# Cross-attention Mamba block and expert layer: placing arithmetic, bias and skip terms, silu batches, TensorE order and scatters rearranged

## Time and profile before

| | DVE | PE | POOL | ACT |
|---|---|---|---|---|
| busy, us of the span of 312.6 | 218.2 | 264.2 | 218.7 | 170.0 |
| busy from 19.68 to 162.0, us of 142.3 | 125.3 | 106.8 | 113.6 | 88.0 |

### The profile page before, as it was taken

The page is one execution under the profiler, slowest core; times in us unless marked ns, Lnnn a source line. Parts: engine busy times, 40 slices in busy tenths (PEclk is TensorE's granted clock), DMA queues, the critical chain, the costliest instruction groups (busy, mean ns, idle before and its releaser), DMA issues. The chain is left out here.

```text
span 312.6 us, 4937 instructions
## 1 busy us (share of the span) xinstructions
PE 264.2 (85%) x1520; PEld 232.9 (75%) x1520; DVE 218.2 (70%) x383; ACT 170.0 (54%) x367; POOL 218.7 (70%) x182
## 2 busy tenths in 40 slices
PE   8969877886957947697699899999999999999960
PEld 7748665755746636576488799999999999999950
DVE  2489999987699788998945346857575757566610
ACT  1678579463893457638404347646473737373410
POOL 1839699959939699698371686677777777777652
PEclk9995989596796976756559999999999999999995
DMA  6459540052001442110055144454555454644011
GB/s 171 172 142 338 167 170 0 3 191 113 0 17 54 163 155 122 51 53 0 34 199 181 64 103 163 176 210 167 209 167 208 166 207 165 208 166 167 33 40 38
DMA packets 14929, 40.24 MB, mean 129 GB/s; under 512 B 2906, under 2 KB 9756, under 8 KB 11968
## 3 DMA queue, kind: packets, MB, share of 16 engines
q1 hardware_dynamic: 11648, 33.02, 31.2%
q0 software_dynamic: 2816, 6.32, 5.8%
q10 hardware_dynamic: 448, 0.70, 0.9%
HBM read 32.58 MB, written 8.49 MB: 131 GB/s over the span
## 5 line engine op out<-in xcount | busy, mean ns | idle before, releaser
L342 POOL TENSOR_TENSOR dbu<-du,bsb 128x1024 f32<-128x1024 f32 x31 | 72.5, 2359 | 6.2 <-ACT bsb L515 3.6
L1131 DVE TENSOR_TENSOR_SCAN h<-ps,dbu 128x512 f32<-128x512 f32 x64 | 74.5, 1206 | 1.1 <-ACT ps L529 0.7
L529 ACT ACTIVATE ps<-delta,anegs 128x255 f32<-128x255 f32 x128 | 53.0, 462 | 7.5 <-DVE h L1131 7.3
L1296 DVE SCALAR_TENSOR_TENSOR htlo<-ps,hthi 128x320 fp32r<-128x320 f32 x64 | 30.5, 487 | 35.2 <-ACT hthi L655 35.2
L766 PE MATMUL ps<-cst,hc 128*128 128x128 f32 x256 | 48.4, 351 | 0.0
L749 PE MATMUL ps<-stack,sels 64*128 64x256 f32 x64 | 19.5, 393 | 33.1 <-DVE hc L1142 29.6
L426 POOL TENSOR_TENSOR w2lo<-w2raw,w2hi 128x512 fp32r<-128x512 f32 x30 | 38.4, 1303 | 9.8 <-ACT w2hi L646 9.6
L766 PEld LDWEIGHTS ps<-cst,hc 128*128 128x128 f32 x256 | 39.4, 182 | 4.6 <-issue 2.2
L749 PEld LDWEIGHTS ps<-stack,sels 64*128 64x128 f32 x64 | 12.3, 239 | 40.6 <-issue 40.5
L935 PE MATMUL ps<-hthi,w2hi 128*128 128x320 f32 x128 | 40.3, 315 | 0.0
L935 PE MATMUL ps<-xthi,w1hi 128*128 (+1 forms) x128 | 40.2, 314 | 0.0
(11 more groups left out here) (149 smaller groups left out, 482.1 us busy)
## 6 DMA issues: line engine op xcount, KB each, us to landing
w1raw<-in_w SPq DMA_DIRECT2D x8, 1024.0 KB
w2raw<-in_w SPq DMA_DIRECT2D x8, 1024.0 KB, 4.8
bsb<-b_rows SPq DMA_DIRECT2D x7, 1024.0 KB, 7.3
expert_rows<-fill SPq DMA_DIRECT2D x1, 2580.0 KB, 15.9
xe<-expert_rows SPq DMA_DIRECT2D x8, 258.0 KB, 5.3
out<-x SPq DMA_DIRECT2D x4, 256.0 KB, 4.9
xnat<-in_x SPq DMA_DIRECT2D x1, 768.0 KB, 7.4
xe<-expert_rows SPq DMA_DIRECT2D x8, 64.5 KB, 5.5
```

The lines of the kernel that those rows point to most:

```text
L342: nc.gpsimd.tensor_tensor(dbu[j % DRING][:], du[:, :, None, cols(b)].to_broadcast([P, EC, 2, L]), bsb[b % 2][:, None, 2 * p:2 * p + 2, :]. ...
L529: ins = nc.scalar.activation(decays(g % SLOTS_DA)[:, c, i * L + 1:(i + 1) * L], delta[:, c, b * L + 1:(b + 1) * L], ACT.Exp, scale=anegs[: ...
L1131: nc.vector.tensor_tensor_scan(h[g % HRING][:, c].rearrange("p n t -> p (n t)"), decays(g % SLOTS_DA)[:, c, :], dbu[g % DRING][:, c].rearr ...
L1296: nc.vector.scalar_tensor_tensor(out=htlo[:, f, :], in0=ps[:, f % 4, 0:CAP], scalar=0.0, in1=hthi[:, f, :].bitcast(F32), op0=ALU.max, op1= ...
```

## The change

- **Placing.** In `place`, three intermediates (`place_of`, the picked products, `slot`) lie in BBANK of PSUM and no longer in SBUF. The softmax weights leave `place`: DVE makes the sum and its reciprocal in a new `sum_weights`, one step later, and ACT multiplies in a new `weigh`.
- **D * u.** ACT writes `skip = u * D` (two instructions a batch) and `open_sums` adds it with four transposes in place of four matmuls (eight passes); `diagd` goes.
- **Bias.** For batches 1 to 3 the bias of dt is loaded on all partitions (`dtb`, one more DMA) and added with four transposes; for batch 0 ACT adds it as the bias of two Abs instructions and DVE in two instructions of 256 columns, from two banks (`first_dt`).
- **silu.** z tiles are silu'd 2, 3, 3 in place of 2, 4, 2.
- **Order on TensorE.** `project(b + 2)` runs at step p = 7 of b. `dt_part` is split over p = 0 and 1. `turn_x1` moves a step earlier, `logits` stays (one later in batch 3), `counts` one later; the turning of z for batch 3 moves from p = 5 to 1, that of x from after the loop's last `c_cast` to p = 5. `choose` follows one step later, `x1_turned` one earlier.
- **Order on POOL and ACT.** Scatters go two at a time at p = 1 and 5 of batch 2, and at p = 2 and 3 of batch 3; those of batch 2's rows come after POOL's four `w1lo`. `z_rstd` and `softplus_delta` come a step later. `split_w1` runs in two halves, at p = 1 and 4.
- **Join.** The four clock-keeping matmuls between `place_rows(0)` and `counts` go, and TensorE waits for the slots after the L1026 matmuls. At the start, 2 and 6 clock-keeping matmuls are added.

```diff
-            keep_clock(4, DABANK)
             counts(B - 1)
             place_rows(1)
-            pe.wait_ge(s["slots_done"], B)
...
@@ start of TensorE
+            keep_clock(2, BBANK)
             pe.wait_ge(s["dts_in"], 16)
...
-            dt_bias(V0BANK)
+            keep_clock(6, BBANK)
...
@@ TensorE's loop
-                if nb < B and p == (0 if b else 1):
...
+                if b >= 1 and nb < B:
+                    if p == 0:
                         pe.wait_ge(s["zt_done"], b)
+                        dt_bias(WBANK)
+                        dt_part(nb, 0, WBANK)
+                    if p == 1:
+                        dt_part(nb, 1, WBANK).then_inc(s["v_psum"], 1)
...
+                if b + 2 < B and p == 7:
+                    if b:
+                        pe.wait_ge(s["slots_done"], b)
+                    project(b + 2, XBANK[b + 2])
-                if b >= 1 and p == (1 if b == B - 1 else 3):
+                if b >= 1 and p == (1 if b == B - 1 else 2):
...
@@ POOL's loop
-                if b == 0 and p == 4:
+                if b == 0 and p == 5:
                     z_rstd(2, slice(BT, TILES))
...
+                if b == 2 and p in (1, 5):
...
+                    send(0 if p == 1 else 1)
+                if b == 3 and p in (2, 3):
+                    send(p)
                 drive(j)
-            send(B - 2)
             for m in range(WP):
...
+            for j in tiles_range(B - 2):
+                send(j)
             row_rstd(B - 1)
             pool.wait_ge(s["xe_in"], 32)
...
@@ ACT
+            def weigh(b):
+
+                act.wait_ge(s["weights_sum"], b + 1)
+                act.wait_ge(s["const_done"], 1)
+                for j in tiles_range(b):
+                    ins = nc.scalar.activation(xrow[:, j, :, DM], etop[:, j, 0:TOPK], ACT.Copy,
+                                               scale=rsum[:, j:j + 1])
+                ins.then_inc(s["gates_done"], 1)
```

More of the change, by code:

```diff
@@ L83, in cols, with tiles_range @@
     return slice(b * L, (b + 1) * L)
+def tiles_range(b):
+    return range(b * BT, (b + 1) * BT)
 def tiles_of(b):
@@ L498, in decay_exps @@
                     act.wait_ge(s["delta_done"], EC * b)
-                nc.scalar.activation(spe, by_chunk(bank), ACT.Abs).then_inc(s["sp_abs"], 1)
-                act.wait_ge(s["sp_abs"], b + 1)
+                    nc.scalar.activation(spe, by_chunk(bank), ACT.Abs).then_inc(s["sp_abs"], 1)
+                else:
+                    for c in range(EC):
+                        nc.scalar.activation(spe[:, c, :], ps[:, bank + c, 0:L], ACT.Abs,
+                                             bias=ch[:, c, DTB:DTB + 1]).then_inc(s["sp_abs"], 1)
+                act.wait_ge(s["sp_abs"], EC + b)
                 nc.scalar.activation(spe, spe, ACT.Exp, scale=-1.0).then_inc(s["sp_exp"], 1)
@@ L597, in _, with skip_rows @@
             decay(1)
+            def skip_rows(b):
+                act.wait_ge(s["u_done"], EC * (b + 1))
+                if b:
+                    act.wait_ge(s["opened"], b)
+                for c in range(EC):
+                    ins = nc.scalar.activation(skip[:, c, :], u[:, c, cols(b)], ACT.Copy,
+                                               scale=ch[:, c, DSK:DSK + 1])
+                ins.then_inc(s["skip_done"], 1)
+            skip_rows(0)
             def silu_pieces(b, bank, tiles, scaled):
@@ L626, in _ @@
                         row_scales(b - 1)
-                        top_exp(b - 1)
                         for j in range((b - 1) * BT, b * BT):
                             normalise(j)
-                if b == B - 1 and p == 5:
-                    for m in range(WP):
-                        split_w1(0, m)
-                if p == (7 if b < B - 2 else 6):
+                    if p == (4 if b == B - 1 else 6):
+                        top_exp(b - 1)
+                    if p == (5 if b == B - 1 else 7):
+                        weigh(b - 1)
+                if b == B - 1 and p in (1, 4):
+                    for m in range(WP // 2):
+                        split_w1(0, m + (WP // 2 if p == 4 else 0))
+                if p == (7, 7, 6, 2)[b]:
                     z_turned(b)
@@ L640, in _ @@
             top_exp(B - 1)
+            weigh(B - 1)
             def split_w2(e, m):
@@ L700, in dt_bias @@
                 for c in range(EC):
-                    nc.tensor.matmul(by_chunk(bank)[:, c, :], dts[0:1, 2 * DI + c * P:2 * DI + (c + 1) * P],
-                                     onesf[0:1, 0:1].to_broadcast([1, L]), start=(c == 0), stop=False,
-                                     skip_group_check=True)
+                    for t in range(BT):
+                        nc.tensor.matmul(by_chunk(bank)[:, c, t * P:(t + 1) * P], dtb[:, c * P:(c + 1) * P], ident,
+                                         start=(c == 0 and t == 0), stop=False, is_transpose=True,
+                                         skip_group_check=True)
             def dt_part(b, k, bank):
@@ L709, in dt_part, with first_dt @@
                                            skip_group_check=True)
+                return ins
+            def first_dt(k):
+                for c in range(EC):
+                    ins = nc.tensor.matmul(ps[:, V0BANK + c, 0:L], wdt[:, k, c * P:(c + 1) * P], u[:, k, cols(0)],
+                                           start=(k == 0), stop=(k == EC - 1))
                 return ins
@@ L1258, in _ @@
                         variance(b - 1, row_stats(b - 1))
-                    if p == (2 if b == B - 1 else 4):
+                if nb < B and p == (2 if b else 3):
+                    softplus_t(nb, WBANK)
+                if b >= 1:
+                    if p == (3 if b == B - 1 else 5):
                         choose(b - 1)
@@ L1272, in _ @@
             place(last)
+            sum_weights(last)
             def metas(e, first):
```

156 lines of the change are left out of this document (80 added, 76 removed).

## The result

Four executions of the changed kernel beside four of the kernel before, on one chip: 300.81 us in the median (300.18 to 302.52) against 314.19 (312.95 to 314.87). The ratio is 0.9587, with a 95% interval of 0.9537 to 0.9637. Forecast were 302.4 us and a range of 296.5 to 309.0. The profiled execution took 300.18 us, its span is 298.4.

What follows compares the result with a forecast made beforehand. DVE was taken as the bound of the batches, busy 125.3 of 142.3 us, with POOL next. The terms summed to -11.9, applied to 314.25, for a forecast of 302.4 us, range 296.5 to 309.0.

Steps and rivals of the forecast that it cites:

- DVE's waits in the steps: Batch steps: waits for `project`, logits and `wgs` go, and one multiply a batch moves to ACT; -14.1 us.
- Last steps: End of batch 3's steps: `mult(31)` no longer waits for the turn and copy of z; -1.9 us.
- The start: Up to scan(0): clock-keeping matmuls fill TensorE's pauses, so batch 0's `dt_part` runs at 2.4 GHz; -1.9 us.
- PSUM intermediates: In `place`: moving three intermediates to PSUM changes DVE's time by 0.1 us at most; taken as 0.
- New wait at scan(9): Batch 1's first steps: later `z_rstd` delays the silus of z, `decay(9)` and so scan(9); +1.3 us.
- Waits not yet seen: Steps: `softplus_t(2)` and `(3)` wait 0.5 each, `c_cast(13)` 0.8 behind `conv` and `logits`; +1.8 us.
- Scatters and the join: Join after mult(31): POOL's later scatters make `xe` land late and TensorE wait 2.7 us at `place_rows(0)`; +0.9 us.
- Clock in the join: Join: TensorE's idle time may drop its clock to 1.2 GHz and lengthen the L1026 matmuls; +1.5 us.
- Expert 1's rows: Expert stage: batch 3's scatters, gated by `weigh`, come 1 us later relative to the first expert; +0.5 us.
- TensorE becomes the bound: Rival, chance 0.04: steps of batches 0 to 2 gain nothing at TensorE's lower clock; 316.5 us, slower.
- Rows late and TensorE cold: Rival, chance 0.17: in the join `xe` lands in 5.4 us and the long idle drops the clock; 308.3 us.
- Rows in time: Rival, chance 0.22: in the join POOL's chain ends sooner or DVE's waits cover it, clock stays; 298.5 us.

Runs made afterwards that it cites:

- the second profile: The changed kernel, unedited, timed and profiled again on another chip; ratio 0.9692 against the kernel before.
- e4: The changed kernel with six clock-keeping matmuls between the logits and TensorE's wait for `xe`; ratio 0.9639 against the kernel before.
- e1: The changed kernel without the 2 and 6 clock-keeping matmuls at the start; ratio 0.9752 against the kernel before.
- e8: The kernel before with clock-keeping matmuls (2 and 2) added in its start; ratio 0.9976 against the kernel before.
- e2: The changed kernel with z's statistics in two steps of three tiles and `z_rstd` two steps sooner; ratio 0.9510 against the kernel before.
- e7: The changed kernel with D times u and the bias by matmuls again, order as changed; ratio 0.9643 against the kernel before.
- e3: The changed kernel with the four scatters of batch 2's rows after the second `w1lo`, not the fourth; ratio 0.9582 against the kernel before.
- e11: The changed kernel with `turn_x1` and `x1_turned` a step later in batches 1 and 2; ratio 0.9838 against the kernel before.

## Why the prediction was right

The sign, the place and the size came out: -11.9 forecast, -14.2 in the profiled span, -13.4 in the medians of the first set and -10.3 in the second. The terms are less exact than the sum: the start's gain has in part another reason, and the last steps, the new waits and the join each came out smaller than forecast.

- **DVE's waits in the steps (-14.1).** Right, and the core of it. Before, DVE stood still for them and was the busiest engine; after, the batches are as long as its work. The `stack` and `top` waits in the steps, 13.0, are gone, and DVE's work in batches 1 and 2 is 0.2 us shorter each, as forecast for `weigh`. The steps in all, with the last steps and the new waits, were to give -12.9 (-14.1 - 1.9 + 1.3 + 1.8) and gave -12.9 in the first profile; that the digits meet is luck, as the second gave -11.2. Undoing `project`'s move costs 5.0 (5.0 forecast). Undoing the turn costs 5.7 and the later `choose` 3.9, 9.6 together against 8.0. The three sum to 14.6, more than the 13 they share. Each may also cover for the others; the clock fell at other times in these profiles, so the surplus is not assigned.
- **Last steps (-1.9).** Smaller in its place: `mult(31)` still waits 0.81 us, for `c_cast(31)`, so 1.1 of its 1.93 is gained. Another 1.0 came at `gate_y` in the join, which waits 1.81 and not 2.77; there the prediction had counted 0.1.
- **The start (-1.9).** Right in number (-2.8 and, in the second profile, -1.95), not in its reason. `dt_part` takes 1.96 or 1.97 us in eleven of twelve profiles with the padding (2.35 in e4), 3.78 and 3.48 without. But "before the slow ones TensorE had pauses" does not hold for the kernel before: its windows have TensorE busy for 2.00 of every 2.00 us from 2 to 14 us, and until 13 us every pass of 256 columns takes the slow 629 ns or more. There the clock had not risen yet. Nor did the record contradict the durations, as the prediction says: in the trace file it begins with the first rise, at 13.9 us in the kernel before, 5.3 in e1 and 3.9 to 6.6 in the twelve padded profiles, and the 1.00 ahead of it is only how the windows print a stretch without an entry. In e8 and in the first profile the rise comes ahead of the padding. So the padding keeps the clock up (e1 puts that at 1.0 us), and much of the rest of this term looks like that one profile's late rise. That the number came out rests here on luck. The Trainium skill, "TensorE: Matmul & The Clock Gate" (Part 1: The HAM clock gate), has the throttled state as the default and activity as what releases it; the slow passes ahead of the first rise agree with the first half, e1 and e4, whose clock fell after pauses, with the second.
- **PSUM intermediates (0).** Right. The three instructions of `place` that write the moved intermediates took 171, 192 and 186 ns each before, and the cast that reads the last one 170; now, from 60 to 150 us (busy us, mean ns of one):

```profile
L1271 DVE TENSOR_REDUCE ps<-ps 128x4 f32<-128x32 f32 x3 | 0.6, 199 | 0.1
L1269 DVE TENSOR_TENSOR ps<-oh,ps 128x32 f32<-128x32 bf16 x3 | 0.6, 195 | 0.1
...
L1267 DVE SCALAR_TENSOR_TENSOR ps<-over,ps 128x16 f32<-128x16 f32 x3 | 0.5, 179 | 0.1
...
L1272 DVE CAST sloti<-ps 128x4 uint32<-128x4 f32 x3 | 0.5, 160 | 0.1
```

  That is 8 ns more for the first (L1267), which read PSUM before as well, 3 and 13 more for the next two and 10 less for the cast. The 65 ns, an estimate from the 58 and 120 cycles of the Trainium skill's "VectorE: DVE Perf Modes" (The TRN2 errata), are not there.
- **New wait at scan(9) (+1.3).** Right: it waited 1.64 us for ACT, behind silus that waited 2.35 for POOL, and batch 0 is 0.9 longer in one profile, 1.95 in the other. e2 takes the wait away.
- **Waits not yet seen (+1.8).** The right places, less in size. `mult(13)` waits 0.62 and 0.73 us for `c_cast(13)` behind `conv` and `logits`, forecast 0.8. `softplus_t(2)` does not wait in either profile and `softplus_t(3)` 0 and 0.39, forecast 0.5 each; with less room (e1, e7) `softplus_t(2)` waits 0.57 and 0.96. That makes 0.6 and 1.1 for the 1.8. `mult(1)` and scan(3) in batch 0, 0.2 and 1.1 together, were not on the list.
- **Scatters and the join (+0.9).** Right chain, three sizes off. The last scatter was issued at E + 1.25 (2.1 forecast), and the two reads of `xe` landed 2.7 and 2.5 us after their issue, less than the 3.2 taken as the least from the earlier trace rows; so `place_rows(0)` began at E + 6.7, not 8.5, after 1.69 us of waiting and not 2.7. From there to the first expert matmul it took 7.66 us, where 5.6 and the clock's 1.5 make 7.1. The join is 1.2 longer than before, where this term and the next had 2.4.
- **Clock in the join (+1.5).** Right in kind, small in size: TensorE did fall to 1.2 GHz after the pause, and e4 puts the price at 2.2 us.
- **Expert 1's rows (+0.5).** Not shown: the experts take 137.38 us before and 137.74 and 137.62 after, and 137.4 to 138.5 in the other kernels.
- **TensorE becomes the bound (0.04).** It did not come: DVE has under 1.2 us of idle time in batches 1 and 2 of both profiles. But the limit of 0.68 was batch 1's work, where the clock was 0.90 and 0.91. Batch 2 fell to 0.66 in the second profile and still took 32.65 us: its work is less, 22.90 us at 0.71, which would fill 32 us only at 0.51. **Rows late and TensorE cold** had the clock right and the landing wrong. **Rows in time** is what e3 makes of the kernel, not what the change did.

The 294.5 for a run with every new wait absent is 294.9 by the prediction's own terms; nothing hangs on it. What stays open: how late the clock rises in other executions of the kernel before, and with it how much of the start's gain is the change's; and how much of the batches' spread between executions is TensorE's clock.

## What to carry to other kernels

List the waits of the busiest engine, with their releasers, and move the releaser's work one step earlier or the waiter one step later. Here three such moves took away 13 us of waits without making anything faster. Look at what stands behind the moved instruction in its queue, as an in-order queue turns a late input into a wait of somebody else (e11). A pause of 2 us on TensorE cost twice here, once as a pause and once as a lower clock: filling it with idle matmuls gave almost as much as removing it (join 12.55 and 11.98 us against 14.78). Before one profile's start is taken as the base of a gain, look when its clock first rises.

## What was not expected of the hardware

- The windows print a granted clock of 1.00 ahead of the record's first entry, a rise that came at 3.9 to 6.6 us in thirteen profiles and at 13.9 in the kernel before. Matmuls tell the true level there: passes of 256 columns take 634 ns before the rise and 379 after it. Once the record has begun it is right: in e1 it reads 0.50 from 8.7 to 12.1 us, over the slow `dt_part`, and in e4 from 7.8 to 11.2.
- The join's two reads of `xe` (258 and 64.5 KB) landed 2.5 to 2.9 us after their issue in the changed kernel's two profiles; in the kernel before the same two took 5.2 and 6.2. The median of all reads of `xe` is 5.4 to 5.6 in both kernels.
- After e3's pause of only 0.30 us, with small bf16 matmuls behind it, the clock fell all the same (0.69 in 156 to 158, 0.50 in 158 to 160); with e4's padding it stayed at 1.00.
